# Four of eight batches by hats and matmuls in every fourth unit, unit 0 placed in two parts, and a new order of the pieces

## What is computed

```
# tokens: 16 rows are one window, 46 windows a batch (750 // 16)
off  = einsum('bwkc,ock->bow', xr, w_off) + b_off      # two offsets for each of 16 taps
px   = window*16 + tap + dx ; x0 = floor(px) ; frac = px - x0
val  = max(0, 1-|dy|) * ((1-frac)*x[x0] + frac*x[x0+1]) # rows outside 0..749 count as 0
tok  = [cls, einsum('bckw,dck->bwd', val, w_def) + b_def] + positional
# attention, one head, with an additive term
h    = tok + softmax(Q K^T/sqrt(128) + W2 tanh(W1q Q + W1k K + b1) + b2) V     # of layernorm(tok)
# experts
out  = h + sum over the 2 best of 8 experts + one shared expert                # of layernorm(h)
```

## Time and profile before

| | us |
|---|---|
| median of 3 runs | 1547.31 (1546.66 to 1550.46) |
| the profiled execution | 1551.96 |
| span of its profile | 1550.2 |
| mean granted clock of TensorE | 0.724 |

### The profile page before, as it was taken

One profiled execution on the slowest core, in us unless ns is written; L12 is line 12 of the kernel. 1 busy time (PEld: TensorE's weight loads), 2 busy tenths in 40 slices (PEclk: granted clock), 3 DMA queues, 4 the chain that ended last, 5 costly groups with the idle time before them and its releaser, 6 DMA issues.

```text
span 1550.2 us, 17047 instructions
## 1 busy us (share of the span) xinstructions
PE 818.0 (53%) x6302; PEld 452.3 (29%) x6302; DVE 606.3 (39%) x1399; ACT 536.9 (35%) x983; POOL 556.8 (36%) x594
## 2 busy tenths in 40 slices
PE   1115343360926538183562927537193663829987
PEld 0003131230514224051331504224051431405554
DVE  3303132250724418062350715327072451706854
ACT  0205051240714326071441606235071432607642
POOL 4760715326071441706235070532607144170000
PEclk8557567575967759586685957769596785958999
DMA  7730304041240513214041230414124051220000
GB/s 177 157 93 11 78 26 101 25 97 45 56 80 15 113 31 71 77 38 91 21 108 38 60 83 20 107 26 102 45 56 80 16 112 32 28 79 5 10 15 11
DMA packets 111584, 94.35 MB, mean 61 GB/s; under 512 B 68396, under 2 KB 99716, under 8 KB 111500
## 3 DMA queue, kind: packets, MB, share of 16 engines
q0 software_dynamic: 18640, 38.08, 13.7%
q1 hardware_dynamic: 88864, 52.00, 12.7%
q10 hardware_dynamic: 3996, 3.17, 0.9%
HBM read 88.74 MB, written 4.43 MB: 60 GB/s over the span
## 4 chain that ended last, share of the span: by engine, by line
another core or an unknown queue 45%; PE 38%; ACT 7%; DVE 4%; issue 3%; ACTq 1%; DMA 1%; SPq 0%; DVEq 0%
PE bank L904 7%; PE bank L782 6%; PE bank L738 6%; PE bank L927 5%; ACT SC L436 2%; PE bank L810 2%; PE bank L757 2%; PE bank L818 2%; PE bank L876 1%; PE bank L859 1%; PE bank L915 1%; ACT HT L386 1%; PE bank L825 1%; PE bank L839 1%
## 5 line engine op out<-in xcount | busy, mean ns | idle before, releaser
L345 POOL DMA_INDIRECT G<-in_x,idx x576 | 551.1, 957 | 834.5 <-DVE idx L529 616.3
L904 PE MATMUL bank<-Z,c_w1e 128*128 128x376 f32 x288 | 148.3, 596 | 349.5 <-ACT HE L467 328.1
L782 PE MATMUL bank<-HT,XN 128*32 128x184 f32 x3072 | 203.6, 344 | 191.4 <-issue 170.4
L467 ACT ACTIVATE HE<-bank,c_fb 128x376 f32<-128x376 f32 x128 | 73.2, 572 | 626.4 <-remote 537.1
L688 DVE TENSOR_TENSOR GE<-HE,bank 128x376 f32<-128x376 f32 x128 | 69.5, 543 | 553.5 <-ACT HE L467 535.1
L782 PEld LDWEIGHTS bank<-HT,XN 128*32 128x32 f32 x3072 | 111.8, 116 | 276.7 <-issue 221.7
L386 ACT ACTIVATE HT<-PXB,c_lneg 128x736 f32<-128x736 f32 x192 | 159.9, 900 | 92.4 <-remote 68.3
L904 PEld LDWEIGHTS bank<-Z,c_w1e 128*128 128x128 f32 x288 | 56.3, 221 | 408.3 <-ACT HE L467 348.0
L393 ACT ACTIVATE HT<-HT 128x2208 f32<-128x2208 f32 x64 | 130.4, 2038 | 1.2
L927 PE MATMUL bank<-GE,c_w2e 128*128 128x376 f32 x256 | 112.0, 535 | 0.0
L738 PE MATMUL bank<-VT,c_wdef 128*128 128x380 f32 x256 | 87.4, 495 | 6.6 <-DVE VT L596 6.6
(11 more groups left out here) (143 smaller groups left out, 958.4 us busy)
## 6 DMA issues: line engine op xcount, KB each, us to landing
xt<-in_x SPq DMA_DIRECT2D x248, 96.0 KB
PXB<-pw SPq DMA_DIRECT2D x16, 768.0 KB
G<-in_x,idx POOLq DMA_INDIRECT x576
XN<-in_x SPq DMA_DIRECT2D x16, 384.0 KB
WYB<-pw SPq DMA_DIRECT2D x64, 48.0 KB
out<-OUTS SPq DMA_DIRECT2D x64, 44.0 KB
est<-SQHC SPq DMA_DIRECT2D x32, 35.2 KB, 2.0
SC<-est SPq DMA_DIRECT2D x16, 69.0 KB
```

Source lines behind the costliest of these rows:

```text
L345: pool.indirect_dma_start(out=G[h][:, col, :], out_offset=None, in_=x.rearrange("b (l c) -> (b l) c", c=C), in_offset=bass.IndirectOffsetO ...
L467: act.activation(HE[e % 4][:, :], cols(2), ACT.Relu, bias=cs["fb1"][:, e:e + 1]).then_inc(he_ready, 1)
L782: mm = pe.matmul(bank[0][32 * g:32 * g + 32, HW * c:HW * c + HW], XN[h][:, b, C * ch + 32 * c:C * ch + 32 * c + 32], HT[half][:, k, g, :], ...
L904: pe.matmul(cols(2), w1e[:, e, :], Z2[h][:, :], start=True, stop=True).then_inc(up_full, 1)
```

## The change

1. In the units 0, 4, 8 and 12 (FULLER) only two pairs of batches are gathered, 24 indirect DMAs; the third pair is dense. Those units have four dense batches: ACT pieces k4 to k11, PE pieces n4 to n7, DVE pieces n2 and n3, own buffers XNE, PXE and WYE, and a second DRAM tensor pwx. The other units skip these pieces.
2. In unit 0 the first pair of batches is placed alone, as soon as its x has come (`first_places` on PE, ACT and DVE; PSUM bank 5), and POOL gathers it on its own signal. The loads of x change queues, the copy of the identity to bf16 comes later, and the setup products move to banks 2 to 4.
3. All four lists are new, and single pieces work on another unit than their letter says (SHIFTED). The four warming matmuls of step 16 are gone.

```diff
+FULLER = (0, 4, 8, 12)
+AHEAD = {"m": 0, "e": 0, "r": -1, "f": -2, "g": -2, "d": -2, "c": 1, "b": 1, "n": 1, "h": 2, "k": 1, "a": 3, "p": 3,
+         "q": 3, "y": 3, "t": 4, "x": 4}
+SHIFTED = {
+    "tensor": {"n0": 2, "m0": 1},
+    "vector": {"n0": 2, "g0": -1, "n1": 2, "m1": 1, "r7": 0, "g1": -1, "r8": 0, "m2": 1, "g2": -1, "m3": 1, "g3": -1, "m4": 1, "r10": 0, "g4": -1, "r11": 0, "n2": 2, "r12": 0, "r6": 0, "c0": 2, "c1": 2, "c2": 2, "r13": 0},
+    "scalar": {"m0": 1, "r6": 0},
+    "sync": {"e0": 1, "e1": 1, "e2": 1},
+}
 ORDER = {
-    "tensor": ("n0 fs gc g0 n1 f0 ds m0 f1 m1 r7 d0 g1 f2 r8 m2 g2 f3 m3 r9 g3 m4 d1 r10 m5 f4 m51 d2 g4 f5 m52 r11 g5 n2 "
-               "f6 r12 g6 d3 f7 g7 d4 d5 n3 d6 b3 d7 d8 a3 a4").split(),
-    "scalar": ("gc fs r6 f0 m0 k0 f1 r7 f2 k1 f3 m3 r9 m41 m4 m5 f4 m51 f5 m52 k2 f6 r12 k3 h0 h1 f7 h2 h3 a3 a4").split(),
-    "vector": ("r6 c0 r7 g0 m1 g1 r8 m2 n0 g2 m3 g3 m4 r10 g4 c1 r11 g5 r12 g6 c2 n1 r13 g7 r14 b3 d8 d9 a4 t0 t1 t2 t3").split(),
-    "sync": ("e0 e1 e2 x0 y0 p0 d9 q0").split(),
+    "tensor": ("gc fs m1 r7 n1 g0 f0 r8 ds m2 r9 f1 m3 n2 g1 r10 m4 f2 n3 d0 g2 m5 m51 f3 n4 m52 d1 r11 n5 f4 g3 "
+               "d2 f5 g4 r12 d3 n6 n7 f6 g5 b3 d4 g6 f7 a3 d5 g7 a4 d6 d7 d8 m0 n0").split(),
+    "scalar": ("k0 gc fs r7 k1 f0 k2 r9 f1 m3 k3 k4 m41 m4 k5 f2 k6 m5 m51 k7 k8 f3 k9 m52 f4 k10 k11 f5 h0 r12 "
+               "h1 h2 f6 h3 f7 a3 r6 a4 m0").split(),
+    "vector": ("n3 g5 r14 b3 g6 r6 g7 a4 d8 r7 d9 c0 m1 r8 n0 m2 g0 c1 m3 g1 m4 r10 g2 c2 n1 g3 n2 r11 t0 g4 r12 "
+               "t1 r13 t2 t3").split(),
+    "sync": ("y0 x0 p0 q0 e0 e1 e2 d9").split(),
 }
...
 def steps(engine, pieces, first, last):
-    u = s + AHEAD[name[0]]
+    u = s + SHIFTED[engine].get(name, AHEAD[name[0]])
...
 def gathers(m, h):
-    pool.wait_ge(idx_ready, u + 1)
-    for bp in range(GP):
+    for bp in range(GP - 1 if u in FULLER else GP):
+        if u == 0 and bp == 0:
+            pool.wait_ge(idx_first, 1)
+        else:
+            pool.wait_ge(idx_ready, u + 1)
...
@@ write_positions
+                if u in FULLER:
+                    v = fuller_before(u)
+                    for r, t in ((1, px[:, GBLK - WG:GBLK, :]), (0, nw[h][:, GBLK - WG:GBLK, :])):
...
@@ hats, dense and dense_out
+            if b >= 2 and u not in FULLER:
+                return
...
@@ dense_out
+            if b == 3:
+                dve.wait_ge(dense_read, dense_before(u + 1))
+                dve.sem_inc(g_free, 1)
+                dve.sem_inc(vt_ready, 1)
...
-            load_first(sp, (0, 1))
+            load_first(sp, (0, 2))
-            load_first(act, (2, 3))
+            load_first(act, (1, 3))
...
-            steps("vector", pieces, -4, -1)
+            turn_x(0)(0, 0)
+            turn_x(1)(0, 0)
+            first_places()
+            turn_x(2)(0, 0)
+            turn_x(3)(0, 0)
+            steps("vector", pieces, -3, -1)
```

More of the change, by code:

```diff
@@ L85, in __call__, with audio_tower @@
         self.eng.wait_ge(self.sem, self.n)
-def audio_tower(nc, x, consts, rows, pw, est, out):
+def audio_tower(nc, x, consts, rows, pw, pwx, est, out):
     fp32, bf16, i32 = mybir.dt.float32, mybir.dt.bfloat16, mybir.dt.int32
@@ L232, in load_first, with fuller_before, dense_before, later @@
                     eng.dma_start(xt[32 * g:32 * g + 32, WG * bp:WG * bp + WG, :], src[g]).then_inc(x_in[bp], 16)
+        def fuller_before(u):
+            return sum(f < u for f in FULLER)
+        def dense_before(u):
+            return 2 * u + 2 * fuller_before(u)
+        def later(u):
+            return WG if u == 0 else 0
         def steps(engine, pieces, first, last):
@@ L476, in _ @@
                       "gc": gc, "fs": shared_hidden, "a3": offsets_out, "a4": row_hats}
-            pieces.update({f"{'hk'[b]}{2 * half + i}": hats(b, half)[i] for b in range(2) for half in range(2) for i in range(2)})
+            pieces.update({f"{'hkkk'[b]}{4 * max(b - 1, 0) + 2 * half + i}": hats(b, half)[i]
+                           for b in range(4) for half in range(2) for i in range(2)})
             pieces.update({f"f{e}": hidden(e) for e in range(E)})
+            first_offsets_out()
             steps("scalar", pieces, -3, -2)
@@ L533, in stage_a, with places @@
+                places(u, a, NBLK, idx_ready, rest_ready)
                 dve.wait_ge(idx_ready, u + 1)
                 chain(dve.tensor_scalar(rowb[:, :], rowb[:, :], float(NB * LP), None, ALU.add))
+            def places(u, a, z, placed, rested):
+                h = u % 2
+                chain(dve.tensor_tensor(px[:, a:z, :], offT[:, a:z, 4:8], base[:, a:z, :], ALU.add))
+                z = min(z, GBLK)
+                pxg, rrg = px[:, a:z, :], rr[:, a:z, :]
+                chain(dve.tensor_scalar(rrg, pxg, -0.5, 0.0, ALU.add, ALU.max))
+                chain(dve.tensor_scalar(rrg, rrg, float(L - 2), ROUND, ALU.min, ALU.add))
+                dve.tensor_tensor(idx[h][:, 4 * a:4 * z].rearrange("p (t n) -> p t n", n=4), rrg,
+                                  rowb[:, a:z].unsqueeze(2).broadcast_to([128, z - a, 4]), ALU.add).then_inc(placed, 1)
+                wait(dve, e_abs, 2 * u)
+                ins = dve.scalar_tensor_tensor(rest[:, a:z, :], rrg, ROUND, pxg, ALU.subtract, ALU.subtract)
+                if rested:
+                    ins.then_inc(rested, 1)
+                else:
+                    chain(ins)
@@ L568, in piece @@
                     u = 2 * m + h
+                    if bp == GP - 1 and u in FULLER:
+                        return
                     if bp == 0:
@@ L572, in piece @@
                                                 nw[h][:, 0:GBLK, :].unsqueeze(3).broadcast_to([128, GBLK, 4, 2]), ALU.mult))
-                    dve.wait_ge(gathered[h][bp], 16 * 4 * WG * (m + 1))
+                    skipped = sum(f <= u and f % 2 == h for f in FULLER) if bp == GP - 1 else 0
+                    dve.wait_ge(gathered[h][bp], 16 * 4 * WG * (m + 1 - skipped))
                     k0 = 4 * WG * bp
@@ L753, in a3, with offsets @@
                 pe.wait_ge(x_turned, 4 * (u + 1))
+                offsets(bank[0], 32 * later(u), XCOLS).then_inc(off_full, 1)
+            def offsets(psum, c, z):
                 for r in range(2):
@@ L768, in piece @@
                     u = 2 * m + h
+                    if b >= 2 and u not in FULLER:
+                        return
+                    rows_, bb = (XN[h], b) if b < 2 else (XNE, b - 2)
                     if half == 0:
-                        if b == 1:
-                            pe.wait_ge(dense_read, 2 * u + 1)
-                        elif isinstance(m, int) and u >= UNITS - 1:
+                        if b:
+                            pe.wait_ge(dense_read, dense_before(u) + b)
+                        elif u >= UNITS - 1:
                             pe.wait_ge(h0_ready, u)
@@ L937, in _ @@
                       "gc": gc, "fs": up(E), "ds": down(E), "d8": d8, "b3": b3, "a3": a3, "a4": a4}
-            pieces.update({f"w{k}": keep_busy for k in range(WARM)})
-            pieces.update({f"n{2 * b + half}": dense(b, half) for b in range(2) for half in range(2)})
+            pieces.update({f"n{2 * b + half}": dense(b, half) for b in range(4) for half in range(2)})
             pieces.update({f"f{e}": up(e) for e in range(E)})
```

152 lines of the change are left out of this document (102 added, 50 removed).

## The result

| | before | after |
|---|---|---|
| median of the runs on one chip | 1547.9 (1546.66 to 1550.46, 4 runs) | 1473.55 (1470.04 to 1475.18, 4 runs) |
| ratio, 95% interval | | 0.9515 [0.9493, 0.9536] |
| profiled execution, its span | 1551.96, 1550.2 | 1470.04, 1468.2 |
| mean granted clock | 0.724 | 0.759 |

The change makes the kernel 4.9% faster.

What follows compares the result with a forecast made beforehand. It took the kernel as bound by alternation: a hold, growing with the gathers, in which PE crawls and signals wait, then a busy stretch. Terms -20 (fuller units), -4 (start), -28 (order) sum to -52: 1495 us, own range 1478 to 1512, 8-in-10 1460 to 1550.

Steps and rivals of the forecast that it cites:

- Fewer gathers: Units 4, 8 and 12 gather 24 instead of 36, taking 17.1 us off each hold (lower end 15.0).
- More dense work: Four more dense half-pieces in each fuller unit: PE +8.3 us, plus 2 us for ACT's tight fit (0 to 6).
- The start: Up to unit 2's first gather: earlier loads and placing one part first bring it from 153.81 to 149.5, -4 us (0 to -12).
- The order: New lists move 2.3 us of PE work out of the bounding stretch; -2 us a period, 14 times, -28 us.
- The warming matmuls: Dropping the four in step 16 costs 0; a slower clock there would cost under a microsecond more.
- The order gives nothing: Rival: PE's pieces only change places because DVE's chain of small steps sets the stretch's length; 1523 us, chance 0.17.
- PE gets on during the gathers: Rival: the new order gives PE some 35 more instructions in the hold, 5 us of full-speed work a period; 1425, chance 0.12.
- DVE becomes the bound: Rival: DVE's work in the stretch grows 3.6 us while its 12.0 us idle stays, +3.6 a period; 1570 us, chance 0.11.
- The hold isn't the gathers': Rival: the hold is PE's own backlog of dense instructions, so 12 fewer gathers free nothing; 1546 us, chance 0.10.
- the spot between g3 and g5: In the stretch, t0 to t3 between experts' products, each holding up a down-projection; where DVE would become the bound.

Runs made afterwards that it cites:

- new_order_no_fuller: The kernel after with no unit of four dense batches, so only the new lists and unit 0's separate placing; 1481.18 us, ratio 0.9577 to the kernel before.
- old_order_first_only: The kernel after with the lists of before and no fuller unit, so only unit 0's separate placing is left; 1546.72 us, ratio 0.9991 to the kernel before.
- old_order_all: The kernel after without the new lists, keeping unit 0's separate placing and the fuller units; 1554.2 us, ratio 1.0043 to the kernel before.
- before_thin_dense: The kernel before with 16 of the 48 matmuls of each dense half, gathers unchanged; 1443.73 us against 1547.59.

## Why the prediction was right, and where it was off

The forecast of 1495 had the side right and was 21 us too high; 1473.55 is inside 1460 to 1550, and 4 us below the forecast's own range of 1478 to 1512. The cause it named, a hold that grows with the number of gathers, stands. Its terms, against the 82 us:

- **Fewer gathers**: -17.1 a unit predicted, -16.5 measured; the release 34 us after the first of 24 gathers predicted, 34.7 measured. (Two readings of the rows were a little off: the earlier trace rows give 44.27 / 35 = 1.265 us from gather to gather, not 1.248, and the clock in a steady hold is 0.58 on average by the earlier trace rows, not 0.50.)
- **More dense work**: 8.3 for PE and 2 for ACT predicted, +11.5 measured. In the dense step PE is busy 9.4 more than in the ordinary one and idle 2.6 more. The three units together -15 for -20, inside the stated -26 to -11, though the upper end was added up wrong: 15.0 for the gathers and 4 us more for ACT make -0.7 a unit, -2 for three. A fourth, unit 0, which I took for free, costs some 6 at the start, as unit 2's first gather at 146.9 in new_order_no_fuller and at 152.9 in the kernel after shows.
- **The start**: "-4 for 153.81", measured -0.9. The first gather at 14 to 16 (15.4), unit 1's at 62 (61.2), the release at 113 (112.2) and the seven hat halves to 145 (144.1) all came as written. The step of the start that failed is the next one, in which ACT takes unit 2's offsets as soon as its hats are done. The timelines of ACT and of PE:

```profile
142.03 2.04 ACT L458 ACTIVATE HT<-HT 128x2208 f32<-128x2208 f32 x1
149.03 0.58 ACT L412 ACTIVATE off<-bank,c_boff 128x384 f32<-128x384 f32 x1 [4.96 <-PE bank L864]
```
```profile
139.53 7.05 PE L846 MATMUL bank<-VT,c_wdef 128*128 128x380 f32 x16 [1.34 <-DVEq L696]
147.41 1.50 PE L864 MATMUL bank<-XT,c_wof 128*32 128x384 f32 x16 [0.82 <-DVE h L706]
```

PE stands before the offset product with b3 of unit 0, for 7.05 us, and ACT waits 4.96. I had costed ACT's queue alone and not asked what PE had ahead of that product, although show the same wait before the change, 3.79 us. With it, 145 + 3.8 + 3.9 gives 152.7 for the first gather of unit 2; 152.9 was measured. (And 145 + 3.9 is 148.9, not 149.5.)

- **The order**: this is the term that was mis-sized most: -28 predicted, -66 measured. I took "-2 us a period, between +3.6 and -5", 14 times. The full periods and the tail gave -3.6 to -4.8 each, -45 for the twelve, for the -24 that 2 us each make. Two things were mis-sized. I had 2.3 us of PE's work leaving the stretch; the earlier trace rows and the ordinary stretch above say 38.48 to 37.46, 1.0 us, at a clock of 0.95 for 0.90. But I had left PE's idle time of 2.4 us where it was, and it is what went: to 0.24 us. Another 0.8 us is in the hold (51.4 to 50.6). And the two early periods, which I had counted at 2 us like the others, gave 21, of which new_order_no_fuller shows 18 with the order alone. Before, step 0's stretch was this:

```profile
205.10:242.50 37.40, 25.76 (x258) 15.91 (x262) 17.25 (x37) 23.95 (x30) 0.03 (x1) 0.76 0.20 57
```

PE was idle for 11.6 us of it; after it is 5.2 of 26.5, with 32 instructions fewer in the stretch. That this is because the step has no experts to put between the small pieces is my reading, no run shows it. I had looked at one steady period and multiplied.

- **The warming matmuls**: put at 0, at most a microsecond. The tails of the profiled executions with the old lists say about 2: 202.4 us with them, 204.9 and 204.3 without (old_order_first_only and old_order_all). In the kernel after it is part of the tail's -4.8.

So the cause of the gain by fewer gathers was right in mechanism and size. For the order only the direction was: the pieces moved behind the positions gave at most a third of what the full stretch gained (1.0 of 3.2 us), and the larger part came from waits that the sum had left as they were. That the time still lies near the forecast is in part luck: the order gave 38 us more than counted, and the dense units and the start gave 8 less.

**The rivals.** *The order gives nothing* (1523) falls by new_order_no_fuller: 66 us. What spoke for it, that a stretch with PE 94% busy has no air to gain, was wrong too: the 2.4 us of idle time went. *PE gets on during the gathers* (1425): its busy time in the hold went from 11.96 to 13.73 and its instructions from 73 to 80, not by 35; n0 ahead of the release helps ACT a little and PE hardly. *DVE becomes the bound* (1570): DVE's busy time in the stretch rose by 2.7, for the 3.6 expected (28.88 to 31.59), but its idle time fell from 12.0 to 6.1, so half of it was not needed; and with PE idle for only 0.24 us, the spot between g3 and g5 doesn't decide. *The hold isn't the gathers'* (1546) falls by the 24-gather windows and by before_thin_dense. The Trainium skill's rule behind it (SBUF — State Buffer, "Who interferes with whom"), that DMAs and compute engines don't contend, agrees with the plain DMAs, which hold nobody, and with the second group; in the first and third group the indirect ones do hold PE (51.2 us for 36 gathers at half the bytes as at all of them), and there the measurement decides. No run shows whether the hold comes about in SBUF.

**What stays open.** Why PE crawls and signals come late while GpSimd issues indirect DMAs, and why it doesn't in one group. The runs narrow it to the indirect form and to a price per gather (51.4 - 34.7 for 12 of them, 1.39 us each; the 72 of the start take 106.4 us, 1.48 each); none shows the path. One hint is in the hold of the kernel after: matmuls of one column (930.39, 0.16 us long) also come up to 1.7 us apart, which speaks for a price of the instruction and not of its work. Whether PE lacks instructions or is kept from starting those it has, no run tells.

## What to carry to other kernels

Before sizing a new order of the work, measure the idle time of the bounding engine in every kind of step, the first and the last ones too: here the two early steps gave as much as half of the eleven full ones. An exchange of one resource for another (gathers for hats) is worth what the order can hide: the same exchange cost 7 us with the old lists and gave 8 to 10 with the new, and in the group without holds seven fuller units took 30 us more than three. And where nothing is busy for half of the time, change one thing at a time (count, bytes, form, the waiting engine's backlog) and look at the release; its distance from the first gather told more here than any total.

## What was not expected of the hardware

The same program, the kernel before, took 1547.5 (1545.08 to 1552.97), 849.67 (847.13 to 854.18) and 1547.59 us (one run) in three groups of runs. The difference is as large as that of the holds: without gathers it takes 844.58 in the third.

In a hold, PE's instructions mostly start at about multiples of 0.70 us from each other. Where it is slowest for long, a matmul comes each 2.80 us, with a weight load halfway (not shown). From the hold of the kernel after:

```profile
953.49 0.47 PE L904 MATMUL bank<-HT,XN 128*32 128x184 f32 x1 [2.33 <-issue]
956.29 0.47 PE L904 MATMUL bank<-HT,XN 128*32 128x184 f32 x1 [2.33 <-issue]
...
970.30 0.46 PE L904 MATMUL bank<-HT,XN 128*32 128x184 f32 x1 [1.64 <-issue]
970.99 0.47 PE L904 MATMUL bank<-HT,XN 128*32 128x184 f32 x1 [0.23 <-issue]
971.68 0.47 PE L904 MATMUL bank<-HT,XN 128*32 128x184 f32 x1 [0.23 <-issue]
972.39 2.72 PE L904 MATMUL bank<-HT,XN 128*32 128x184 f32 x30 [0.24 <-issue]
```

The same matmul is issued 30 times in 2.72 us as soon as the hold is over. An indirect DMA takes POOL 0.94 us and 0.30 behind it, a plain one of the same size 0.53 in all; against plain DMAs, a gather with its hold costs the kernel (1547.59 - 834.47) / 576 = 1.24 us more.
